# Query stacks from DRAM, key parts in stack order, an earlier fourth key split

## What is computed

```python
# B=8 batches, x (8,112,256), context (8,375,256)
x = x + tanh(g_xattn[0]) * align(ctx, layernorm(x))        # time-warping path, 112 x 375
x = x + tanh(g_ffn[0])   * bitffn(layernorm(x))            # ternary weights, conv of 3, silu, 1024 hidden
x = x + tanh(g_xattn[1]) * attention(layernorm(x), ctx)    # 16 heads of 16, softmax over 375 keys
x = x + tanh(g_ffn[1])   * patterns(layernorm(x))          # gelu, mean over tokens, three top-k rounds
# attention:
q = (query @ Wq.T + bq) * 16**-0.5 ; k = key @ Wk.T + bk ; v = value @ Wv.T + bv
out = softmax(q @ k.T) @ v ; return out @ Wo.T + bo
```

## Time and profile before

| | us |
|---|---|
| median of 3 runs | 645.31 (644.6 to 645.93) |
| the profiled execution | 645.01 |
| its span, first to last instruction | 643.3 |
| PE busy | 428.2 (67%) |
| DVE busy | 430.2 (67%) |
| ACT busy | 273.0 (42%) |
| POOL busy | 99.4 (15%) |
| DMA queue of SP, share of 16 engines | 35.3% |
| granted clock of TensorE, mean | 0.782 |

### The profile page before, as it was taken

How to read it: one execution, slowest core, us unless ns; L and a number is a source line. 1 busy time by engine, 2 the same in 40 slices (tenths; PEclk the granted TensorE clock), 3 DMA queues, 4 the chain that set the end, 5 groups by cost and what they waited for, 6 DMA issues and landing times.

```text
span 643.3 us, 10182 instructions
## 1 busy us (share of the span) xinstructions
PE 428.2 (67%) x3448; PEld 306.5 (48%) x3448; DVE 430.2 (67%) x1714; ACT 273.0 (42%) x635; POOL 99.4 (15%) x201
## 2 busy tenths in 40 slices
PE   2998799622392403657989888899999655406306
PEld 2667685511272103635767666677455553106303
DVE  4645999799736896868776676775454665473573
ACT  4744544812303861024455454665533452351340
POOL 7900000000052561335800000000000000000000
PEclk9998699755585855667798898999999887855556
DMA  4560004292006992002699794700300361000001
GB/s 133 153 162 1 2 1 154 65 207 77 2 1 107 136 135 24 1 1 60 158 128 176 118 218 52 72 2 1 121 11 2 119 218 56 2 0 1 1 1 58
DMA packets 45770, 47.16 MB, mean 73 GB/s; under 512 B 5198, under 2 KB 43927, under 8 KB 44695
## 3 DMA queue, kind: packets, MB, share of 16 engines
q1 hardware_dynamic: 45718, 46.51, 35.3%
HBM read 37.80 MB, written 8.60 MB: 72 GB/s over the span
## 4 chain that ended last, share of the span: by engine, by line
PE 54%; DVE 25%; ACT 9%; issue 6%; SPq 3%; DMA 2%; POOL 0%; DVEq 0%; ACTq 0%
PE ps L1959 7%; PE ps L1913 4%; PE ps L1900 4%; PE ps L1889 4%; DVE PR L980 4%; ACT below L1594 4%; PE ps L1735 4%; PE ps L1743 3%; PE ps L1875 3%; SPq L548 3%; PE ps L1799 3%; PE ps L2085 2%; DMA ctxP<-in_ctx 2%; DVE prod L976 2%; PE ps L1694 2%
## 5 line engine op out<-in xcount | busy, mean ns | idle before, releaser
L1141 DVE TENSOR_REDUCE negm<-ps 112x1 f32<-112x375 f32 x128 | 66.3, 544 | 21.5 <-PE ps L1889 18.4
L1565 ACT ACTIVATE E<-ps 125x448 f32<-125x448 f32 x96 | 52.1, 543 | 57.0 <-PE ps L1900 56.8
L1889 PE MATMUL ps<-ks,qs 96*112 96x375 bf16 x128 | 46.6, 378 | 13.6 <-issue 10.2
L2058 PE MATMUL ps<-cnt,same 128*128 128x3 bf16 (+4 forms) x40 | 6.9, 173 | 61.8 <-ACT below L1594 43.4
L1913 PE MATMUL ps<-E,v 125*32 125x112 f32 x768 | 42.9, 275 | 0.0
L1900 PE MATMUL ps<-qs,ks 99*125 99x112 bf16 x384 | 41.0, 232 | 0.9 <-ACT E L1565 0.5
L1900 PEld LDWEIGHTS ps<-qs,ks 99*125 99x125 bf16 x384 | 35.3, 144 | 10.0 <-issue 6.7
L1129 DVE TENSOR_REDUCE acts<-gel 128x4 f32<-128x448 f32 x32 | 19.8, 620 | 29.3 <-ACT gel L1528 29.3
L2058 PEld LDWEIGHTS ps<-cnt,same 128*128 128x128 bf16 (+1 forms) x40 | 4.4, 110 | 65.1 <-issue 65.1
L727 POOL CAST kp<-kx 128x750 bf16<-128x750 f32 x8 | 6.5, 811 | 168.7 <-ACT path L1477 143.0
L1889 PEld LDWEIGHTS ps<-ks,qs 96*112 96x112 bf16 x128 | 17.7, 142 | 25.3 <-issue 19.4
(11 more groups left out here) (363 smaller groups left out, 1129.9 us busy)
## 6 DMA issues: line engine op xcount, KB each, us to landing
ks<-key_parts SPq DMA_DIRECT2D x48, 187.5 KB, 8.5
piw<-fn_process_input_weights SPq DMA_DIRECT2D x8, 1024.0 KB, 4.9
key_parts<-kp SPq DMA_DIRECT2D x16, 281.2 KB, 4.7
ctx_again<-in_ctx SPq DMA_DIRECT2D x7, 512.0 KB
ctxP<-in_ctx SPq DMA_DIRECT2D x8, 375.0 KB
keys<-kx SPq DMA_DIRECT2D x16, 187.5 KB, 2.2
kx<-keys SPq DMA_DIRECT2D x8, 375.0 KB, 6.6
patn<-in_L_ffn_input_patterns SPq DMA_DIRECT2D x1, 2048.0 KB, 17.8
```

Source lines behind the costliest of these rows:

```text
L1141: drain(dve.tensor_reduce(negm[:, n:n + 1], bank(nm)[0:S, 0:SC], AX.X, ALU.max, negate=True), nm)
L1565: drain(fn(E[:, (KCH * f + c) % 6, :], bank(nm)[0:KC, 0:4 * S], ACT.Exp), nm)
L1889: fill(mm(bank(nm)[0:S, 0:SC], qs[0:SR, u // 4 % 3, n, :], ks[0:SR, u // 4 % 3, n, :], start=True, stop=True), nm)
```

## The change

- `key_parts` in DRAM is laid out part, row of the head, head, key. `load_stack` then reads runs of 16 x 375 elements; `store_parts` writes six DMAs per batch, one for each part and tile.
- The query stacks are no longer made by PE, except for batch 0 (steps `u` 0 to 3). SP stores the parts of a half (four batches) to `query_parts` with six DMAs and reads them back with six, into `qs[0]` (batches 0 to 3) and `qs[1]` (4 to 7), which now hold four batches each.
- POOL splits batch 3 directly after batches 0 to 2. SP stores it there; its stack is loaded in the loop over `b`, after step 3, and the second half of the queries behind it.
- The three rows of the maximum become twelve (`MR`): the row of maxima of four heads is one product of 112 x 12 instead of four of 112 x 3, and the rows of ones on the side of the keys become a block pattern (`kones`), made on POOL behind `joinF` and `joinG`. ACT, not DVE, copies the row.
- The four maximum products of a step go in pairs to two PSUM banks each, and DVE reduces two at a time.
- `patn`, `oiwn`, `opat` and `pval` are loaded behind other stacks than before: `patn` behind that of batch 4, `oiwn` behind 6, the last two behind 7.

```diff
@@ -147,11 +148,11 @@
     for f in range(-LAG - 1, 4 * B + 4):
-        if 0 <= f + LAG + 1 < 4 * B:
-            p.add(("qstack", f + LAG + 1), 3)
+        if 0 <= f + LAG + 1 < 4:
+            p.add(("qstack", f + LAG + 1), 4 + (f + LAG + 1) % 2)
         if 0 <= f + LAG < 4 * B:
-            for i in range(4):
-                p.add(("smax", f + LAG, i), (4 * (f + LAG) + i) % 3)
+            for i in range(2):
+                p.add(("smax", f + LAG, i), 2 * i, 2 * i + 1)
         if 0 <= f < 4 * B:
...
@@ -369,12 +369,12 @@
         qp = rt.take("qp", [128, 2, 3, TOK], BF16)
-        qs = rt.take("qs", [128, 3, NH, S], BF16)
+        qs = [rt.take("qs0", [128, NH, HB * S], BF16), Region(queries_at).take("qs1", [128, NH, HB * S], BF16)]
         negm = rt.take("negm", [S, NH])
         negp = rt.take("negp", [S, 2, NH, 3], BF16)
         pvs = rt.take("pvs", [128, 4 * S])
         rs = rt.take("rs", [S, NH])
-        o = rt.take("o", [S, NH, HD])
+        o = actscr[0:S, :].rearrange("p (n e) -> p n e", n=NH)
         oT = rt.take("oT", [128, DH, S])
...
@@ -520,6 +523,11 @@
             return t[:, 0:B * n].rearrange("p (b n) -> p b n", b=B)
+        def queries_of(u, heads):
+            b = u // 4
+            return qs[b // HB][:, heads, S * (b % HB):S * (b % HB) + S]
...
@@ -582,11 +590,9 @@
-                sp.wait_ge(parts_stored[b % 2], 32 * (b // 2 + 1))
+                sp.wait_ge(parts_stored[b % 2], 96 * (b // 2 + 1))
                 for j, part in enumerate(K_PARTS):
-                    sp.dma_start(ks[HD * j:HD * j + HD, b % 3, :, :],
-                                 key_parts[b, part].rearrange("(n d) s -> d n s", d=HD)
-                                 ).then_inc(stack_loaded[b % 3], 16)
+                    sp.dma_start(ks[HD * j:HD * j + HD, b % 3, :, :], key_parts[b, part]).then_inc(stack_loaded[b % 3], 16)
...
@@ -599,37 +605,65 @@
                 for t in range(2):
-                    sp.dma_start(key_parts[b, :, 128 * t:128 * t + 128, :].rearrange("c p s -> p c s"),
-                                 kp[:, b % 2, t, :, :]).then_inc(parts_stored[b % 2], 16)
+                    for c in range(3):
+                        sp.dma_start(key_parts[b, c, :, 8 * t:8 * t + 8, :].rearrange("d n s -> n d s"),
+                                     kp[:, b % 2, t, c, :]).then_inc(parts_stored[b % 2], 16)
             for i in range(4):
                 sp.wait_ge(keys_stored[i], 64)
             load_keys(0)
             load_keys(1)
             sp.wait_ge(x_ready, B)
-            sp.wait_ge(consts_ready, 1)
+            sp.wait_ge(kones_ready, 1)
             for b in range(3):
-                sp.dma_start(ks[SR:SR + 3, b, :, :], onesb[0:3, :].unsqueeze(1).broadcast_to([3, NH, SC])
+                sp.dma_start(ks[SR:SR + MR, b, :, :].rearrange("p (g i) s -> p g (i s)", i=4),
+                             kones[:, :, :].rearrange("p i s -> p (i s)").unsqueeze(1).broadcast_to([MR, NH // 4, 4 * SC])
                              ).then_inc(loaded["ones_k"], 16)
-            for b in range(3):
+            for b in range(4):
                 store_parts(b)
                 load_keys(b + 2)
-                load_stack(b)
-            for b in range(3, B):
+                if b < 3:
+                    load_stack(b)
+            def store_queries(half):
+                for t in range(2):
+                    sp.wait_ge(q_split, 2 * half + t + 1)
+                    for c in range(3):
+                        sp.dma_start(query_parts[half, c, :, 8 * t:8 * t + 8, :].rearrange("d n s -> n d s"),
+                                     qp[:, t, c, 448 * half:448 * half + 448]).then_inc(queries_stored[half], 16)
+            def load_queries(half):
+                sp.wait_ge(queries_stored[half], 96)
+                lo = S if half == 0 else 0
+                for j, part in enumerate(Q_PARTS):
+                    sp.dma_start(qs[half][HD * j:HD * j + HD, :, lo:HB * S], query_parts[half, part, :, :, lo:HB * S]
+                                 ).then_inc(loaded[f"q{half}"], 16)
+            store_queries(0)
+            load_queries(0)
+            store_queries(1)
+            for b in range(4, B):
                 store_parts(b)
                 if b + 2 < B:
                     load_keys(b + 2)
-            for b in range(3, B):
+                if b == 5:
+                    wait_filled(sp, ("scoreT", 3, KCH - 1))
+                    load_stack(3)
+                    sp.wait_ge(queries_stored[0], 96)
+                    wait_filled(sp, ("qstack", 3))
+                    load_queries(1)
+            for b in range(4, B):
                 wait_filled(sp, ("scoreT", 4 * b - 9, KCH - 1))
                 load_stack(b)
-                if b == 3:
+                if b == 4:
                     sp.wait_ge(x_ready, 2 * B)
                     sp.dma_start(patn[:, :, :], pat_in.rearrange("(c p) d -> p c d", p=128)).then_inc(loaded["pat"], 16)
-                if b == 4:
+                if b == 6:
                     sp.dma_start(oiwn[:, :, :], oiw_in.rearrange("(c p) d -> p c d", p=128)).then_inc(loaded["oiw"], 16)
-                if b == 5:
-                    sp.dma_start(opat[:, :, :], opat_in.rearrange("(c p) d -> p c d", p=128)).then_inc(loaded["opat"], 16)
-                    sp.dma_start(pval[:, :, :], pval_in.rearrange("(c p) d -> p c d", p=128)).then_inc(loaded["pval"], 16)
+            sp.dma_start(opat[:, :, :], opat_in.rearrange("(c p) d -> p c d", p=128)).then_inc(loaded["opat"], 16)
+            sp.dma_start(pval[:, :, :], pval_in.rearrange("(c p) d -> p c d", p=128)).then_inc(loaded["pval"], 16)
             sp.wait_ge(x_ready, 3 * B)
...
@@ -711,6 +745,16 @@
             pool.memset(warm[:, :], 0.0).then_inc(meet_ready, 1)
+            wait_filled(pool, "joinF")
+            wait_filled(pool, "joinG")
+            did(pool.memset(kones[:, :, :], 1.0))
+            settle()
+            did(pool.affine_select(out=kones[:, :, :], in_=kones[:, :, :], compare_op=ALU.is_ge, fill=0.0, base=0,
+                                   pattern=[[-3, 4], [0, SC]], channel_multiplier=1))
+            settle()
+            pool.affine_select(out=kones[:, :, :], in_=kones[:, :, :], compare_op=ALU.is_ge, fill=0.0, base=2,
+                               pattern=[[3, 4], [0, SC]], channel_multiplier=-1).then_inc(kones_ready, 1)
             for k in range(2):
...
@@ -1133,13 +1177,14 @@
                 u = f + LAG
-                for i in range(4):
+                for i in range(2):
                     if u < 4 * B:
                         nm = ("smax", u, i)
                         wait_filled(dve, nm)
-                        n = 4 * (u % 4) + i
-                        drain(dve.tensor_reduce(negm[:, n:n + 1], bank(nm)[0:S, 0:SC], AX.X, ALU.max, negate=True), nm)
-                    if i == 1 and b >= 0 and t == 1:
+                        n = 4 * (u % 4) + 2 * i
+                        drain(dve.tensor_reduce(negm[:, n:n + 2], psum[0:S, 2 * i:2 * i + 2, 0:SC], AX.X, ALU.max,
+                                                negate=True), nm)
+                    if i == 0 and b >= 0 and t == 1:
...
@@ -1148,19 +1193,12 @@
                                  ALU.mult), nm)
-                    if i == 1 and b >= 0 and t == 3:
+                    if i == 0 and b >= 0 and t == 3:
                         nm = ("wo", b)
                         wait_filled(dve, nm)
                         dve.wait_ge(bias_added, b + 1)
                         stt(x[:, b, :], bank(nm)[0:S, 0:D], tg[0:S, 1:2], x[:, b, :],
                             ALU.mult, ALU.add).then_inc(x_ready, 1)
-                    if i == 2 and 0 <= f + 1 < 4 * B:
-                        nm = ("negT", f + 1)
-                        wait_filled(dve, nm)
-                        n = 4 * ((f + 1) % 4)
-                        drain(dve.tensor_copy(qs[SR:SR + 3, (f + 1) // 4 % 3, n:n + 4, :].rearrange("p n s -> p (n s)"),
-                                              bank(nm)[SR:SR + 3, 0:4 * S]), nm)
                 if t == 0 and 1 <= b <= B - 1:
...
@@ -1551,12 +1589,17 @@
                         drain(fn(oT[:, :, :].rearrange("p h s -> p (h s)"), bank(nm)[:, 0:DH * S], ACT.Copy), nm)
-                    if c == 2 and u < 4 * B:
+                    if c == 2 and u < 4:
                         nm = ("qstack", u)
                         wait_filled(act, nm)
-                        n = 4 * (u % 4)
-                        drain(fn(qs[0:SR, u // 4 % 3, n:n + 4, :].rearrange("p n s -> p (n s)"),
-                                 bank(nm)[0:SR, 0:4 * S], ACT.Copy), nm)
+                        drain(fn(qs[0][0:SR, 4 * u:4 * u + 4, 0:S],
+                                 bank(nm)[0:SR, 0:4 * S].rearrange("p (n s) -> p n s", n=4), ACT.Copy), nm)
+                    if c == 2 and 0 <= f + 1 < 4 * B:
+                        nm = ("negT", f + 1)
+                        wait_filled(act, nm)
+                        n = 4 * ((f + 1) % 4)
```

(38 more changed lines are left out.)

29 lines of the change are left out of this document (16 added, 13 removed).

## The result

| | before | changed | changed, run again |
|---|---|---|---|
| median (lowest to highest), us | 645.62 (644.6 to 647.45) | 654.54 (653.06 to 658.07) | 651.99 (650.23 to 658.45) |
| ratio to before on the same chip, 95% | | 1.0151 [1.0113, 1.0188] | 1.0109 [1.006, 1.0157] |
| profiled execution: span, us | 643.3 | 656.2 | 650.5 |

A forecast was written before the change was run, and what follows sets the result against it. It took the attention loop as bound by a ring of 14.1 us stack load and 5.6 us TensorE work. From 645.0 us, +13 (batch 3 split), +2 (kones) and +6 (loop) gave 666.0 us; range 628 to 684, the forecast's own 650 to 684.

The forecast's parts named there:

- Part 2: Feed-forward stage: splitting batch 3 before POOL's adds delays the first add; +13 us, bounds +10 and +19.
- Part 3: POOL's kones memset and selects after the joins slow DVE's chain beside them; +2 us, bounds 0 and +7.
- Part 1: Stack loads with 12,000 B runs stay near 100 GB/s, set by 16 SBUF rows; gain 0 to 0.9 us.
- the start of the loop: Attention loop, step 4 waits for queries stored and reloaded through DRAM; first score product +3 us.
- the long turn at step 16: Stack 4's load queues behind stack 3, the second query load and stores of batches 6 and 7; +11.0 us.
- the ring: Mid-loop, a stack load, then TensorE work until the next may start: 18.2 us per batch instead of 18.8.
- My sign of being wrong: The prediction is wrong if a stack load lands under 9 us after its issue.
- The price of the stores: Key stores, six DMAs per batch with heads outermost: 200 GB/s, 2.9 us instead of 2.2.
- parts 1, 3, 4 and 5: All but the early batch 3 split: kones +2 us, loop +6 us including its late start.
- Both rivals that gave run length a part: Stack loads speed up: to 267 GB/s, 620 us, chance 0.12; or to 200 GB/s, 629 us, chance 0.09.
- half relief: Loads into different row groups overlap at 200 GB/s, a stack in 5.8 us; loop -26, total 629 us; chance 0.09.
- 18 us for products: Attention loop: allowance for removed TensorE products, out of 20 us from 26 x 0.59 + 32 x 0.15.

The follow-up runs named there:

- E10: Changed kernel, batch 3 split after the adds, TensorE stacking queries of batches 0 and 1, stores of batches 6 and 7 first, 32-row loads: 628.14 us, 0.973.
- e9: Kernel before with only the new key_parts layout, and four of six stack parts loaded as two DMAs of 32 rows: 635.26 us, 0.9822.
- e3: Changed kernel with twelve useless products added per step from step 4 on: 653.19 us, 1.0108 of the kernel before.
- e4: Changed kernel with TensorE making the query stacks of batches 0 and 1, not only 0: 649.93 us, 1.0023 of the kernel before.
- e6: Changed kernel with stores and key loads of batches 6 and 7 ahead of stack 3 and the second query load: 653.46 us, 1.0072 of before.

## Why the prediction was right or wrong

**Part 2 (+13), right.** The undone edit gave 9 to 12 us, the path from third split to first add grew by 9.7 and 9.5 us (the rows of before said 10.2), and POOL's row order was as written. Where the whole stretch is read, +12.1 and +16.1, the first add also carries what came before it: the third split itself starts 2.4 us later, in the repeat 6.5, of which part 3 accounts for some 2 and the rest is open.

**Part 3 (+2), right as far as a trace can show.** DVE's timeline of the changed kernel beside POOL's selects:

```profile
116.71 1.48 POOL L753 TENSOR_SCALAR_AFFINE_SELECT kones<-kones 12x1500 bf16<-12x1500 bf16 x1
118.26 1.46 POOL L756 TENSOR_SCALAR_AFFINE_SELECT kones<-kones 12x1500 bf16<-12x1500 bf16 x1
```

```profile
116.64 0.16 DVE L997 TENSOR_TENSOR least<-least,other 128x1 f32<-128x1 f32 x1
...
117.03 1.17 DVE L997 TENSOR_TENSOR least<-least,other 128x1 f32<-128x1 f32 x1
118.24 1.54 DVE L1004 SCALAR_TENSOR_TENSOR which<-total,least,row_id 128x47 f32<-128x47 f32 x1
```

The same operation takes 0.16 us alone and 1.17 us beside a select. The second takes 1.54 us where before it had 0.27, and a third, after the memset of `steps` began, 0.56 instead of 0.25: 1.01 + 1.27 + 0.31 = 2.6 us. No run took this term out by itself. The runs agree with it as far as they go: the first add starts between 211.0 and 213.4 us in the four kernels without `kones`, and between 215.0 and 215.9 in the five with `kones` and a late split.

**Part 1 (rate stays at 100 GB/s), wrong, and the step on which the size failed.** I compared copies that differed in rows and in run length together, and gave all of the difference to the rows. Layout alone is worth 10 us where I had written at most 0.9 us per stack. All later terms used that rate: the start of the loop (+3, measured +0.4 and +1.1 from the first query split, +0.9 and -0.4 from the first add), the long turn at step 16 (+11, measured 5.6: 375.96 - 301.07 = 74.9 us after the first query split against 357.80 - 288.53 = 69.3) and the ring (18.2 us per turn; in the repeat the three turns take 47.2 us together, not 54.6). That the first execution took 54.2 us for them, and +2.0 for the stretch where +3 was forecast, is luck: its clock was 0.76, for which the sum had no term. The order of the queue behind the long turn was right: the one large wait of the loop is where I put it, 7.21 and 9.62 us. My sign of being wrong, a stack load landed under 9 us after its issue, was badly set: the last packet of the stack issued at 338.06 in the changed kernel ends 9.5 us after that, and yet the rate had changed. The price of the stores erred the other way (156 GB/s for 200), by 0.8 us a batch; it stands inside the 9.7 us above.

**The sum without part 2.** I had parts 1, 3, 4 and 5 at +8 (2 + 6). The runs have -10 for the layout and +8 for the rest, -2 together. The 10 us between +8 and -2 are the forecast's error; 21 - 10 = 11 stands against 6 to 9 measured, which the intervals (0.4% and more each) allow.

**The rivals.** Both rivals that gave run length a part were right in this, and half relief (200 GB/s) came nearer in size. That loads into different groups of rows run at once, as it had it, the trace doesn't bear out: there is one round after another, at 131 GB/s, and rounds overlap at most at their edges. Its 629 us had a second fault: it counted 18 us for products that TensorE no longer does (26 steps in the text, but steps 4 to 31 are 28). E10 shows what these are worth when loads hardly hold the loop. From first score to first pattern product it takes 125.36 us, 4 us less than e9's 129.37, although 24 steps are rid of 0.74 us each by the prediction's own price, 17.8 us. TensorE's 119.22 us at a clock of 0.84 would be 105.4 at e9's 0.95; so the clock accounts for the rest by arithmetic, though the two kernels differ in more than the products. The prediction took its steps at the pace of the rows of before and had no term for a lower clock: the second step that failed. In the changed kernel, where loads hold the loop as well, it moved the total by no more than the runs can tell (e3).

**Open.** The stretch after the loop is 2.0 and 2.3 us shorter in the changed kernel; in the other runs it takes 192 to 197 us without order, so this may be scatter. The 8 us that the rest of the change costs were split only in part: e4 gives back 6 to 8 of them, e6 2 to 5, and these overlap.

## What to carry to other kernels

Before a rate is given to the number of rows of a DMA, find two transfers that differ in rows alone; here long runs and more rows both helped, and together took a 1.15 MB load from 100 to 197 GB/s. A pattern in short windows can be one of counting: halve the windows before you read a mechanism into it. A step that is moved earlier on an engine's queue costs what stands behind it: check when its data lands, not only how long it takes. And don't count TensorE's removed products at their old duration: look at the granted clock that the thinner stretch will get, and find out with a kernel that does only the thinning.

## What the runs showed of the hardware

TensorE stood at 1.2 GHz for 41 us while reported busy for 38 of them. Removing small products lowered the mean clock of a stretch from 0.94 to 0.87, adding them raised it from 0.84 to 0.95, and TensorE's busy time moved by 3.3 us and 0.2 us of some 120. Six DMAs of 16 rows with runs of 12,000 B, one behind the other on a queue of their own, moved at 131 GB/s in the steady part (145 with the first round counted) against 100 with runs of 750 B. Six stores with 8 heads outermost in DRAM moved 156 GB/s with a DMA share of 0.50.
